# Three expert groups of 6, 6 and 4 batches in place of four, and the key root on ScalarE, in a two-layer block kernel

## The reference

```
scores = sigmoid(x @ gate_w); topk_w, topk_i = top_k(scores, 6); topk_w /= sum(topk_w)
routed = sum over the 6 experts e of topk_w[e] * (silu(x @ wg[e]) * (x @ wu[e])) @ wd[e]
shared = silu(x @ sg) * (x @ su) @ sd
```

## Time and profile before

| what | us |
|---|---|
| median of 3 runs (lowest, highest) | 2054.55 (2050.47, 2056.04) |
| the profiled execution's own time | 2047.37 |
| its span, from the first to the last instruction | 2045.5 |
| busy in the span: PE, weight loads, DVE, ACT, POOL | 1523.8, 1146.5, 1123.0, 877.0, 940.2 |
| mean granted TensorE clock, share of full speed | 0.887 |

### The profile page before, as it was taken

How to read it: one execution, slowest core, us unless ns; L and a number is a source line. 1 busy time by engine, 2 the same in 40 slices (tenths; PEclk the granted TensorE clock), 3 DMA queues, 4 the chain that set the end, 5 groups by cost and what they waited for, 6 DMA issues and landing times.

```text
span 2045.5 us, 46039 instructions
## 1 busy us (share of the span) xinstructions
PE 1523.8 (74%) x15344; PEld 1146.5 (56%) x15344; DVE 1123.0 (55%) x2910; ACT 877.0 (43%) x1789; POOL 940.2 (46%) x1246
## 2 busy tenths in 40 slices
PE   3755857787788887887878777797977877788840
PEld 2433545554466666676666656565764666566630
DVE  5565556657555655556465656566555555524332
ACT  2441433353355454553544444453643545355520
POOL 3335062534425154425336455546646456625555
PEclk8777988899899999998999988898998989899975
DMA  6986641413334425353344535364463644546643
GB/s 151 238 212 170 152 112 22 112 45 93 99 87 130 111 90 124 110 125 101 102 105 136 116 122 132 117 144 123 134 150 105 140 127 110 162 125 187 190 141 93
DMA packets 467085, 258.04 MB, mean 126 GB/s; under 512 B 231537, under 2 KB 454321, under 8 KB 466865
## 3 DMA queue, kind: packets, MB, share of 16 engines
q1 hardware_dynamic: 399696, 178.00, 33.8%
q0 software_dynamic: 22784, 54.55, 9.6%
q10 hardware_dynamic: 44384, 22.55, 3.9%
HBM read 127.28 MB, written 127.40 MB: 125 GB/s over the span
## 4 chain that ended last, share of the span: by engine, by line
PE 38%; issue 15%; DVE 14%; POOL 10%; another core or an unknown queue 6%; DMA 5%; SPq 3%; ACT 3%; DVEq 0%; ACTq 0%; POOLq 0%
PE s3r L1636 11%; POOL rt L817 4%; PE s2m L1636 4%; POOL yard L933 2%; PE s3r L1939 2%; PE s1b L1706 2%; PE s3r L1963 2%; SPq L652 2%; DVE th L1486 2%; DMA yard<-y_d,slot 2%; PE s2r L1814 2%; DVE mx L1285 2%; POOL h3l L913 2%; DVE m L1366 1%
## 5 line engine op out<-in xcount | busy, mean ns | idle before, releaser
L913 POOL TENSOR_TENSOR h3l<-th,h3h 96x256 f16<-96x256 f32 (+2 forms) x288 | 199.2, 693 | 602.7 <-ACT h3h L1140 600.1
L1486 DVE SCALAR_TENSOR_TENSOR th<-th,s3r 96x256 f32<-96x256 f32 (+2 forms) x288 | 119.4, 415 | 288.1 <-ACT th L1135 259.8
L933 POOL DMA_INDIRECT yard<-y_d,slot x192 | 192.6, 1003 | 85.8 <-issue 39.9
L1140 ACT CAST h3h<-th 96x256 f16<-96x256 f32 (+2 forms) x288 | 116.5, 405 | 247.8 <-DVE th L1492 124.0
L889 POOL DMA_INDIRECT rows_d<-rows,slot x192 | 188.1, 980 | 67.7 <-issue 66.8
L1366 DVE TENSOR_REDUCE m<-s2r 128x3 f32<-128x384 f32 x256 | 135.4, 553 | 151.2 <-remote 99.3
L1636 PE MATMUL s3r<-yard,xg 128*128 128x128 f16 x1920 | 183.1, 227 | 46.8 <-DVE th L1492 20.6
L1127 ACT COPY yard<-s3r 128x1024 f16<-128x1024 f16 x160 | 162.2, 1014 | 63.1 <-remote 36.4
L1636 PE MATMUL s3r<-yard,xu 128*128 128x128 f16 x1920 | 181.1, 225 | 3.0 <-issue 2.9
L1636 PEld LDWEIGHTS s3r<-yard,xg 128*128 x1920 | 133.0, 101 | 77.4 <-issue 63.6
L1135 ACT ACTIVATE th<-s3r 96x256 f32<-96x256 f32 (+2 forms) x192 | 72.8, 379 | 217.7 <-PE s3r L1636 179.8
(11 more groups left out here) (326 smaller groups left out, 3705.0 us busy)
## 6 DMA issues: line engine op xcount, KB each, us to landing
yard<-rows_d SPq DMA_DIRECT2D x160, 256.0 KB
y_d<-yard SPq DMA_DIRECT2D x160, 256.0 KB
rows_d<-share ACTq DMA_DIRECT2D x21, 1024.0 KB, 6.8
part_d<-part SPq DMA_DIRECT2D x32, 512.0 KB, 3.6
stacks<-part_d SPq DMA_DIRECT2D x192, 64.0 KB
land<-part_d SPq DMA_DIRECT2D x96, 64.0 KB
part<-part_d SPq DMA_DIRECT2D x96, 64.0 KB
x<-in_L_attn_x SPq DMA_DIRECT2D x16, 256.0 KB, 2.6
```

The lines of the kernel that those rows point to most:

```text
L913: g.tensor_tensor(h3l[0:m, n % 2, :], th3[0:m, n % 2, :], h3h[0:m, n % 2, :], ALU.subtract).then_inc(sem("low3"), 1)
L933: g.indirect_dma_start(got4[:, n % RING4, :], None, y_d[k][:, :], bass.IndirectOffsetOnAxis(ap=slot4[:, b, t, j:j + 1], axis=0)).then_inc( ...
L1140: s.copy(h3h[0:m, n % 2, :], th3[0:m, n % 2, :]).then_inc(sem("high3"), 1)
L1486: v.scalar_tensor_tensor(h, h, 1.0, bk[0:m, 0:2 * P], ALU.add, ALU.mult).then_inc(sem("gate3"), 1)
```

## The change

It has four parts. The groups are of 6, 6 and 4 batches, which gives 52, 52 and 40 units, 144 in all, with a new `QUOTA`. The root of `rt2` is taken by ACT (`Sqrt` with a scale of 1/L, in a stage of its own between `x2h` and the Exp of the logits) and DVE (`reciprocal`, right ahead of the spreading); POOL's power and DVE's scaling go. The orders of all five engines are new. And since both buffers of `rows_d` now hold 52 units, the zeroing takes 13 DMAs for each.

```diff
-GROUPS = (5, 4, 4, 3)
-QUOTA = {6: 11, 7: 12, 8: 12, 9: 11, 10: 10, 11: 10, 12: 10, 13: 10, 14: 13, 15: 13, 16: 14, 17: 34}
+GROUPS = (6, 6, 4)
+QUOTA = {7: 9, 8: 9, 9: 9, 10: 9, 11: 8, 12: 8, 13: 13, 14: 13, 15: 13, 16: 13, 17: 40}
...
-            gp.wait_ge(*event("var2_made", it, 1))
-            g.tensor_tensor(rt2[:, :, :], rt2[:, :, :], less_half[:, :].unsqueeze(2).to_broadcast([P, T, H]), ALU.pow).then_inc(sem("root2"), 1)
-            yield
...
+            act.wait_ge(*event("var2_made", it, 1))
+            s.activation(rt2[:, :, :], rt2[:, :, :], ACT.Sqrt, scale=1.0 / L).then_inc(sem("root2"), 1)
+            yield
             act.wait_ge(*fullm(it, "logit"))
...
-            v.tensor_scalar(rt2[:, :, :], rt2[:, :, :], 0.0, L * EPS, ALU.max, ALU.add).then_inc(sem("var2_scaled"), 1)
-            dve.wait_ge(*event("var2_scaled", it, 1))
-            v.tensor_scalar(rt2[:, :, :], rt2[:, :, :], 1.0 / L, None, ALU.mult).then_inc(sem("var2_made"), 1)
+            v.tensor_scalar(rt2[:, :, :], rt2[:, :, :], 0.0, L * EPS, ALU.max, ALU.add).then_inc(sem("var2_made"), 1)
             yield
             dve.wait_ge(*event("root2", it, 1))
+            v.reciprocal(rt2[:, :, :], rt2[:, :, :]).then_inc(sem("rs2_made"), 1)
+            dve.wait_ge(*event("rs2_made", it, 1))
             dve.wait_ge(*event("row_low", it, 1))
             v.tensor_copy(rw2, rt2[:, :, :].unsqueeze(3).to_broadcast([P, T, H, HD])).then_inc(sem("rs2_made"), 1)
...
-            pe.wait_ge(*event("rs2_made", it, 1))
+            pe.wait_ge(*event("rs2_made", it, 2))
```

The strings of `ORDERS` are replaced as a whole. The end of POOL's string (4 is a step of gather and mixing, 3 a step of the ring, the last 3 is the last unit; a batch has 13 steps of stream 4) shows the difference at the end of the program:

```diff
-344344344434434443433343444444444444444444444444444444444440012345677
+344434434443443444343334434444444444444444444444444444444444444444444444444444444444444440012345677
```

More of the change, by code:

```diff
@@ new lines @@
+        "11133333033213333338830030331331181133211113133013323388333033003133833111111211133313302338833033100333238111"
+        "11111313332313883033338133023300331111111113332388331033338303333330033133111331121131314333343333033323333188"
+        "33334040033333313381133121111331133334043331233883300033338331331111111133124334133338283313323334843333333333"
+        "43343333833233833333338333333333333333433433333333333343343333333333833334334333333333333334334333333333333343"
+        "433344444444401234678"
@@ new lines @@
+        "33300332337737373733333333223333003237737737333333322332337733337700337333332233323773377373333003333443444344"
+        "44343443333333223443444333433400323434344344377377337344344344433434443434332323334444300323444377374373733444"
+        "34433333444244243444477337737333324443332243443443444344344433343377373737332333444344434434443433443434444344"
+        "34443433434434443444344434333443443444344344434333443443444344344434333443444444444444444444444444444444444444"
+        "4444444444444444444444444440012345677"
@@ L70 @@
[L70 to L74, removed]
@@ new lines @@
+        "88888882888881122811881882281132111211811313800311011313013033333323388888828823888882288382888833823111110081"
+        "10181101130113313111131133333338888888828888811288218188881228113211121138113138001101131301033333332333888888"
+        "28828888822388288888283300838000111111111111111111118881883333333888333883833333388333333828333332323338323323"
+        "88288833323333383333330033833311333311331331130111011331133130113331131133333333333888388333233833883882382388"
+        "38822383288338828330033333833111331133113811333031301103311313311331131313333333333338883382838388388238328838"
@@ new lines @@
+        "82283388211881138132331100831313833330331301131131333113113013133333333333338883388383883328833888323288331181"
+        "88122881328113311281333383110013113031101131331333303333333333333233888383838882882383882288288833882833383338"
+        "11133111131133131111313333113111001333303388830883833833803883238388332882333838832882382283338333333333333331"
+        "13111113333300311101103333313331313388831331303331183183318333388333883338383383333883323383338823332833833233"
+        "23833323332333833300333333333383303111330331133113011111331131333311331131331333333333333338883338832338338833"
@@ new lines @@
+        "88238233883233288332833883882381100181133308333113011330333311133311313311311133133883838838338833838383388338"
+        "83328338888111381312281133311822321112113133111111333333333333333233332288833338383832388233883888333238833383"
+        "88333883833338333383233333333333333333333333333333333333333888333388333383333883833383333833333883333333883333"
+        "83333883833383333833333333333383333833333333333333333333333333333333333333333333333333333333333333333333333333"
+        "3333333330011234788"
@@ L99 @@
-        "444444444444444444444444444001123478"
+        "16161155556111131131551131131155113335555000550550130555535313113311111111111111111122232222727002213377007100"
+        "88388038838888888838838733222112132112118211721100112112118110018303070337778838818888888838811118838171131131"
+        "11111111111222832220020072832823107030388178878878838838888887811131121131221121131121121182317130023002280807"
+        "03331887887887388388188118818818711111311311111111212232820020027283228317003078818788788388388888887831131321"
@@ L122 @@
+        "33333333333333333333333333333333333333333333333330011234578"
     ),
```

96 lines of the change are left out of this document (36 added, 60 removed), and 4 rows, old and new, of the table PER.

## The result

The changed kernel has a median of 1937.95 us (1933.76 to 1939.87, 4 runs) where the kernel before, in the same comparison, has 2055.30. The ratio is 0.9429, with a 95% interval of 0.9404 to 0.9454: 5.7% faster, 117 us. The forecast was 2014 us, 41 us faster. Its profiled execution took 1936.35 us, with a span of 1934.6 us. POOL's lines are 3 lower than before: the scatter is line 886, the gather 930, POOL's half of a unit 910, the accumulating DMA 919. The Sqrt is line 1064, the reciprocal 1337.

What follows compares the result with a forecast made beforehand. No engine was taken as full: engines hand work on in fixed orders, and one late step stops all. -69 + 63 - 3 - 32 = -41 us from 2047.4 gave 2006.4, plus 7.2 a median of 2014 us; 8-in-10 range 1978 to 2062.

Steps and rivals of the forecast that it cites:

- More behind the last batch: Tail after the last root: 53 units instead of 48 and a last group of 4 batches instead of 3; 63 us paid.
- Fewer units beside the batches: Ahead of batch 15's root: 21 units go, at 3.3 us each; 69 us saved (58 to 90).
- The root: Root on ACT and DVE instead of POOL's power in 16 batches: 2.0 us each, 32 us saved (0 to 62).
- The fear about the bank `mid`: Logits' Exp, late behind Sqrt and table loads, empties `mid` late for the keys: PE's transposes gain 1.5 us, not 3.85.
- the 6.4 us: Sign at the root: the prediction is wrong if PE's transposes come later than this behind the clamp.
- The new orders: New stage orders of the engines: priced at 0 by themselves, their possible effect left to the range.
- One change of group fewer: Two group changes instead of three, each 6 us, partly covered by a batch in the middle: 3 us saved (0 to 6).
- four more zeroing DMAs: 1 MB each, prolonging the zeroing into batch 1 and after: 0 us, at worst 27 if all were waited for.
- the middle gives little: Rival, chance 0.15: attention stages set the batch's pace, a unit taken from the middle gives 1.0 us; 2062 us.
- The root gives nothing: Rival, chance 0.15: two table changes and the held bank `mid` eat the root's 5.4 us; 2046 us.
- The middle is held by PE: Rival, chance 0.2: a removed unit gives its whole 4.31 us, or Sqrt needs no table load; 1993 or 1984 us.
- 104 to 107: Sign in the profile after: us per batch between the roots of batches 5 and 15, from 112.8 less 6 to 9.

## Why the prediction was wrong, point by point

The size was wrong by 76 us; the direction was right. Step by step:

- **More behind the last batch, 63 us paid: right.** Measured 64.2, with the last stretch at 119.5 us for 118.4 and 53 units behind the root as counted. Hardly anything lies beside this work, so rows of before could simply be added up. Some luck is in the close sum: two gathers more behind the last unit (2.5 us) against steps that each came 0.3 to 0.8 us shorter, and 4 more units between the roots where 5 were counted.
- **Fewer units beside the batches, 69 us saved: the step failed.** It took the difference between a batch with units and one without, 2.75 us per unit, as the price of removing one. Emptied in fixed orders, a unit gave 0.3 to 0.9 us. The lower figures are hardly told from nothing, and the emptied units kept their DMAs and handoffs, so a whole unit's price is not measured. The contrast compares two kinds of batch, each with orders laid for it; it does not tell what lighter work returns in orders that stay. It also had a flaw: 5 of the units fall at the end of the window called free of them. The traces have 111 and 91 units ahead of the last root, 20 fewer and not 21. Yet the middle fell by 121 us, which is the next two points.
- **The root, 32 us saved (0 to 62): under-sized.** Alone it gave 51 us, on the common chip 45, while DVE's wait fell from 75.5 to 23.8 and 23.1 us. What failed is pricing it by the distance from the clamp to PE's transposes, 2.0 us a batch. The fear about the bank `mid` was right for the old orders, in which PE stands 27.2 us for the late Exp, and the root still gave more than 32; in the new orders PE has other work until then. In 8 of 16 batches the transposes do come later behind the clamp than the 6.4 us that the forecast named as a sign against it (15.6 and 34.1 us in two of them), though the median is the 6.6 us given above. The idle time that ended at the power would have come nearer than the path's length, but the runs give no rule that turns it into time. In the new orders the same root is worth 82 to 88 us, above the range's end. There DVE's remaining wait and PE's wait for the Exp are both covered; that this is the reason is argued, not shown.
- **The new orders, "priced at 0": the step that failed most.** With the new root in both, groups and orders together give 77 us on one chip (2010.1 to 1933.0), where the forecast had 9 (69 + 3 - 63). Of it 39 us are lost when only the front goes back to the old order, and 1.6 to 1.9% when DVE's cover is taken away; these two may overlap. The front is 54 us shorter up to root 5 (44 with the new root in both, 596.0 to 551.7), with only 5 units fewer to explain it. Since the tail costs 64, everything ahead of it gave some 140 us, and lighter work in orders that stay gives only 6 to 18 of them. How the rest, most of it between roots 5 and 15, divides between fewer units, larger groups and new orders stays open.
- **One change of group fewer, 3 us; four more zeroing DMAs, 0.** Neither was separated. The 26 DMAs take 6.6 us each and root 0 is 7.8 us later; root 1 is 27 us earlier, so if anything waits for them it is made up there.

Of the rivals, *the middle gives little* was right about the unit (1.0 us forecast, 0.7 measured in the kernel before) and wrong about the time, because it too left the orders at nothing. *The root gives nothing* fell, although PE does stand for the late Exp in the old orders. The Trainium skill's page "ScalarE: Activation LUTs" has about 2.66 us for a switch of tables, a drain included, in "What ACT_TABLE_LOAD costs". The trace does not agree: a load ends at 330.81, the Sqrt runs until 331.05, and the next load starts at 331.07 and ends 1.28 us later, with the Exp at 332.36, so a switch is 1.28 us here, and the run without them is no faster. *The middle is held by PE* came nearest in time, for another reason. A batch of the middle took 100.6 us, where the forecast looked for 104 to 107.

## What to carry to other kernels

When all engines work through written orders, the idle time that ends at a stage is a better first look at what shortening it can return than its length is, if all engines are looked at, and lighter work alone returned almost nothing here while the orders stayed. So a change of orders is not to be priced at 0: look for the waits of all batches that a stage ends (here 75.5 us on one line), and ask whether the new order puts work between the request and the use on the requesting engine without making the next engine late. Then look where each wait went: one that is gone from its line can stand again at another line of the same engine (25.1 us at line 1394). A sum of such waits is no price, and a move that pays with one latency can cost with another (36 to 44 us gained with the slow root, 26 lost with the quick one).

## What had not been expected of the hardware

Emptying work seems to have lowered the granted clock a little. The clock of a stretch is a mean over parts at 1.2 and at 2.4 GHz. The profiles show 0.92 to 0.89 in the kernel before, and 0.94 to 0.91 between 600 and 1660 us in the old orders with the new root, where a mean matmul went from 93.1 ns (879.01 us by 9441) to 97.1 ns (858.51 by 8843), with PE's busy share 83% and then 81%. But these are single executions, and they overstate it. Over whole runs on one chip, the median clock of the kernel before was 0.880 (0.875 to 0.888) and with emptied units 0.877 (0.865 to 0.881), while the single profiles of the two had 0.887 and 0.872. Across chips the medians are 0.899 and 0.894 without and 0.886 with emptied units in the old orders with the new root, and 0.898 to 0.901 against 0.891 in the kernel after. Windows of the two kernels in old orders with the new root, without and with the emptied units:

```profile
600.00:1660.00 1060.00, 879.01 (x9441) 683.27 (x9439) 640.21 (x1683) 548.41 (x1107) 478.57 (x712) 0.94 0.47 126
```

```profile
600.00:1660.00 1060.00, 858.51 (x8843) 655.29 (x8844) 620.73 (x1703) 518.19 (x1116) 430.29 (x674) 0.91 0.46 121
```

In the kernel after the middle runs at 0.95, higher than in these, although it has fewer units: PE is 84% busy there, where it was 81% in the kernel before.
